# Later rows and weights requested behind an expert's issued scatters, the last multiply in halves, the last tile turned inside the products ahead

## What is computed

```python
x = x + tanh(g_xattn[0]) * xattn(layernorm(x), ctx)     # softmax over 64 masked keys, then @ Wo + bo
xf = layernorm(x)
probs = sigmoid(xf @ gate_w.T)
top_vals, sel = top_k(probs, 2)
weights = top_vals / (top_vals.sum(-1) + 1e-6)
ranks = cumsum(onehot(sel))[sel] - 1                    # place in the expert's list
valid = ranks < 320
padded[expert, rank] = xf                               # rows gathered by expert
h = gelu(padded @ w1[e]); y = h @ w2[e]
x = x + tanh(g_ffn[0]) * sum_k weights_k * y[slot_k]    # 0 where the slot is not valid
```

## Time and profile before

| | |
|---|---|
| median of 3 executions | 338.8 us (338.32 to 339.88) |
| the profiled execution, its own time | 339.9 us |
| its span in the profile | 338.2 us |
| busy share of the span: PE, PEld, DVE, ACT, POOL | 91%, 79%, 74%, 61%, 57% |
| bytes moved by DMA | 45.68 MB, mean 135 GB/s |

### The profile page before, as it was taken

One profiled execution on the slowest core, in us unless ns is written; L12 is line 12 of the kernel. 1 busy time (PEld: TensorE's weight loads), 2 busy tenths in 40 slices (PEclk: granted clock), 3 DMA queues, 4 the chain that ended last, 5 costly groups with the idle time before them and its releaser, 6 DMA issues. The chain is left out here.

```text
span 338.2 us, 6265 instructions
## 1 busy us (share of the span) xinstructions
PE 308.3 (91%) x2077; PEld 267.3 (79%) x2080; DVE 251.2 (74%) x585; ACT 207.9 (61%) x570; POOL 191.4 (57%) x242
## 2 busy tenths in 40 slices
PE   8989999999999999998849999999999999999800
PEld 3646779988888888887724899999999999999700
DVE  2679887698989898989755398888888888887200
ACT  2646877887888888866461376666666666665300
POOL 8034566585777777788771023555555555566650
PEclk9999999999999999999978999999999999999965
DMA  6989999700111111111224737878787878853440
GB/s 159 274 241 292 182 167 152 195 19 16 49 49 55 57 57 64 56 51 62 78 95 149 249 104 201 204 205 208 204 216 211 224 202 220 211 82 43 48 46 8
DMA packets 40906, 45.68 MB, mean 135 GB/s; under 512 B 5461, under 2 KB 34666, under 8 KB 40874
## 3 DMA queue, kind: packets, MB, share of 16 engines
q1 hardware_dynamic: 33410, 35.78, 39.3%
q0 software_dynamic: 7424, 9.48, 15.6%
q10 hardware_dynamic: 40, 0.02, 0.0%
HBM read 28.02 MB, written 17.24 MB: 134 GB/s over the span
## 5 line engine op out<-in xcount | busy, mean ns | idle before, releaser
L554 POOL DMA_INDIRECT out_dram<-wqT,diag x48 | 73.3, 1528 | 77.4 <-DMA out_dram<-wqT,diag 43.4
L1370 PE MATMUL ps_scores<-value_t,score_t 128*128 128x320 f32 x384 | 59.1, 310 | 0.0
L1370 PEld LDWEIGHTS ps_scores<-value_t,score_t 128*128 128x128 f32 x384 | 56.5, 188 | 0.4 <-DVE value_t L1079 0.3
L1269 PE MATMUL ps_out<-value_t,pT 128*128 128x256 f32 x384 | 53.3, 289 | 0.9 <-DVE pT L968 0.9
L1240 PE MATMUL ps_scores<-score_t,xn 128*128 128x512 f32 x192 | 53.9, 426 | 0.0
L1269 PEld LDWEIGHTS ps_out<-value_t,pT 128*128 128x128 f32 x384 | 47.7, 189 | 1.7 <-issue 1.6
L1240 PEld LDWEIGHTS ps_scores<-score_t,xn 128*128 128x128 f32 x192 | 36.4, 190 | 6.8
L713 ACT ACTIVATE ps_scores<-ps_scores 128x640 f32<-128x640 f32 x30 | 20.6, 688 | 34.2 <-PE ps_scores L1370 34.1
L460 POOL DMA_INDIRECT padded<-z,slot_row x32 | 33.4, 1043 | 10.0 <-issue 7.1
L640 ACT ACTIVATE probs<-ps_scores,row_low 128x64 f32<-128x64 f32 x128 | 38.0, 327 | 0.5 <-DVE row_low L941 0.5
L1093 DVE CAST value_t<-ps_scores 128x640 fp32r<-128x640 f32 x30 | 24.7, 824 | 18.0 <-ACT ps_scores L713 17.8
(11 more groups left out here) (210 smaller groups left out, 690.0 us busy)
## 6 DMA issues: line engine op xcount, KB each, us to landing
raw<-in_L_ffn_w_dram SPq DMA_DIRECT2D x16, 512.0 KB, 4.8
wo_sb<-in_L_ffn_w_dram SPq DMA_DIRECT2D x16, 512.0 KB, 3.5
padded<-empty SPq DMA_DIRECT2D x2, 2064.0 KB, 31.0
diag<-padded SPq DMA_DIRECT2D x16, 258.0 KB, 4.9
out_dram<-x SPq DMA_DIRECT2D x16, 128.0 KB, 1.7
padded<-empty SPq DMA_DIRECT2D x1, 1032.0 KB, 34.1
diag<-padded SPq DMA_DIRECT2D x16, 64.5 KB, 4.7
wq_sb<-in_L_xattn_Wq_dram SPq DMA_DIRECT2D x2, 512.0 KB, 8.0
```

Of the source, the lines that this page charges most:

```text
L554: pool.indirect_dma_start(out, bass.IndirectOffsetOnAxis(ap=xg[0:SLOTS[k], r, k, TOKEN:TOKEN + 1].bitcast(U32), axis=0), y[0:SLOTS[k], j, ...
L1269: op = pe.matmul(ps_attn, pT[:, a, c], mv, start=c == 0 and (a, b) == PARTS[0], stop=c == HC - 1 and (a, b) == PARTS[-1])
L1370: op = pe.matmul(ps_scores[:, f, 0:CAPACITY], w1_hl(p, a)[:, c, f * P:(f + 1) * P], x_hl(p, b)[:, c], start=c == 0 and (a, b) == PARTS[0], ...
```

## The change

It has four parts.

1. **Requests of SP.** In a step e >= 1 SP first waits on a new semaphore `issued` until POOL has issued the three scatters of expert e-1 (POOL writes one column of `sent` behind them), then requests the rows of expert e+3, then w1 of expert e+4, then w2 of expert e+3. In the steps before that, w1 goes ahead of w2. The tail part of the rows counts on a semaphore of its own, `tailed`, which PE's turn doesn't wait for. The 64 third rows of expert 0 are requested by ACT.
2. **The last multiply in halves.** The probabilities of tile 15 are multiplied by their norm on POOL in two halves of 8 heads (`last_multiply`) in place of one multiply on DVE, and the norm is made in halves (`last_norm`). PE turns them in two halves.
3. **The last tile turned and counts made inside the products ahead.** `turn_probs(15)` and `counts(6)` stand inside the products of tile 14, `turn_x1(14)` and `router(14)` inside those of tile 15, which write another bank (ps_misc), read copies of their own (`pT_last`) and don't wait for tile 14's residual. Filler multiplies go from 5 and 3 to 2.
4. **The norms from tile 12 on.** DVE makes the negated mean and the variance plus epsilon (two small instructions in `second_stats`), POOL only the reciprocal root, and ACT the shift (`shift`). POOL's `second_norm(14)` and `second_norm(15)` stand between the dispatches of pair 6; one `mark_tokens` stands a step earlier. On DVE the token weights (`weigh`) are computed behind the counts' inputs, and `first_residual(14)` goes behind the placing of pair 6.

```diff
             def expert(e, j, i):
 
+                if e >= 1:
+                    sp.wait_ge(issued, e)
+                    fetch(e + 3)
+                n = e + 4
+                if 2 <= n < EXPERTS:
+                    sp.wait_ge(w1_low, n - 1)
+                    sp.dma_start(raw1[:, n % 2], w1_load[n]).then_inc(w1_loaded[n % 2], 16)
                 n = e + 3
                 if 2 <= n < EXPERTS:
                     sp.wait_ge(w2_low, n - 1)
                     sp.dma_start(raw2[:, n % 2], w2_load[n]).then_inc(w2_loaded[n % 2], 16)
-                n = e + 4
-                if 2 <= n < EXPERTS:
-                    sp.wait_ge(w1_low, n - 1)
-                    sp.dma_start(raw1[:, n % 2], w1_load[n]).then_inc(w1_loaded[n % 2], 16)
-                if e >= -1:
+                if -1 <= e < 1:
                     fetch(e + 3)
...
                     pool.indirect_dma_start(out, ...).then_inc(added[j], 16)
+                if e < EXPERTS - 1:
+                    pool.memset(sent[:, e:e + 1], 0.0).then_inc(issued, 1)
...
+            def last_multiply(h):
+                p, at = LAST % 2, 8 * h
+                pool.wait_ge(norm_ready, TILES + h)
+                pool.tensor_tensor(probs[:, p, at:at + 8], probs[:, p, at:at + 8],
+                                   norm[:, p, at:at + 8, None].to_broadcast([P, 8, KEYS]), ALU.mult).then_inc(normed, 1)
+
             dispatch(PAIRS - 3, 0, (0,))
+            last_multiply(0)
             second_norm(LAST - 2)
+            last_multiply(1)
             dispatch(PAIRS - 3, 0, (1,))
             dispatch(PAIRS - 3, 1)
             mark_tokens(PAIRS - 2)
             mark_tokens(PAIRS - 1)
+            pool.wait_ge(slots_ready, PAIRS - 1)
+            dispatch(PAIRS - 2, 0, (0,))
             second_norm(LAST - 1)
-            pool.wait_ge(slots_ready, PAIRS - 1)
-            dispatch(PAIRS - 2, 0)
-            dispatch(PAIRS - 2, 1)
+            dispatch(PAIRS - 2, 0, (1,))
+            dispatch(PAIRS - 2, 1, (0,))
             second_norm(LAST)
+            dispatch(PAIRS - 2, 1, (1,))
...
-            keep_busy(5)
-            attend(LAST - 1, {HC // 2: lambda: router(LAST - 2)})
-            turn_probs(LAST)
-            counts(PAIRS - 2)
-            turn_x1(LAST - 1)
-            keep_busy(3)
-            attend(LAST, {HC // 2: lambda: router(LAST - 1)})
+            keep_busy(2)
+            router(LAST - 2)
+            attend(LAST - 1, {HC // 2: lambda: turn_probs(LAST), HC - 1: lambda: counts(PAIRS - 2)})
+            attend(LAST, {3: lambda: turn_x1(LAST - 1), HC - 2: lambda: router(LAST - 1)})
```

More of the change, by code:

```diff
@@ L273, in build @@
         fetched = [sem(f"fetched{k}") for k in range(GATHERS)]
+        tailed = [sem(f"tailed{k}") for k in range(GATHERS)]
         added = [sem(f"added{k}") for k in range(2)]
@@ L539, in _ @@
                 dispatch(PAIRS - 1, k)
-            pool.memset(sent[:, :], 0.0).then_inc(rows_sent, 1)
+            pool.memset(sent[:, EXPERTS - 1:], 0.0).then_inc(rows_sent, 1)
             for k in range(2):
@@ L598, in _, with copy_probs @@
                 job(n, *JOBS[n])
-            def copy_probs(t):
-                for h in range(2):
+            def copy_probs(t, halves=(0, 1)):
+                for h in halves:
                     act.wait_ge(turned, 2 * t + h + 1)
-                    if h == 0:
+                    if t == LAST:
+                        act.wait_ge(scored, 2 * TILES)
+                    elif h == 0:
                         wait(act, attended, t)
-                    act.activation(pT[:, 0, 4 * h:4 * h + 4].rearrange("p c n -> p (c n)"), ps_pT[:, h],
+                    act.activation(pT_of(t, 0)[:, 4 * h:4 * h + 4].rearrange("p c n -> p (c n)"), ps_pT[:, h],
                                    ACT.Copy).then_inc(p_high, 1)
@@ L612, in second_rows @@
                 act.wait_ge(ln2_ready, t + 1)
+                bias = l2[:, p, 2:3]
+                if t >= LATE_TILE:
+                    bias = shift[:, p]
+                    act.activation(bias, l2[:, p, 2:3], ACT.Copy, scale=l2[:, p, 1:2]).then_inc(shifted, 1)
+                    act.wait_ge(shifted, t - LATE_TILE + 1)
                 if t >= RING:
@@ L705, in expert @@
                 if e == -1:
+                    for k in range(2):
+                        act.wait_ge(dispatched[k], 64 * PAIRS // 2)
+                    act.dma_start(xg[0:SLOTS[2], 0, 2], padded[2 * P:CAPACITY, :]).then_inc(fetched[0], 16)
                     for t in range(2):
@@ L891, in step @@
                 if exists(t3):
[L892 to L893 removed]
+                    if t3 < LATE_TILE:
+                        wait(dve, ln2_ready, t3 - 1)
+                        dve.bn_aggr(mv2[:, p3], stats2[:, :]).then_inc(stats2_ready, 1)
+                    else:
+                        second_stats(t3)
                 if route:
@@ L1213, in turn_probs @@
                 for h in range(2):
+                    if t == LAST and h == 1:
+                        pe.wait_ge(normed, TILES + 1)
                     wait(pe, p_low, 2 * (t - 1) + h + 1)
@@ L1259, in attend @@
             def attend(t, between):
-                wait(pe, x1_ready, t)
+                if t < LAST:
+                    wait(pe, x1_ready, t)
                 for c in range(HC):
@@ L1268, in attend @@
                         mv = value_w[b][:, batch_of(t), c]
-                        op = pe.matmul(ps_attn, pT[:, a, c], mv, start=c == 0 and (a, b) == PARTS[0],
+                        op = pe.matmul(attn_of(t), pT_of(t, a)[:, c], mv, start=c == 0 and (a, b) == PARTS[0],
                                        stop=c == HC - 1 and (a, b) == PARTS[-1])
@@ L1314, in step @@
                 if counted_here and r >= LATE_PAIR:
-                    between[HC - 2] = lambda: counts(r)
+                    between[HC // 2 + 1] = lambda: counts(r)
                 if exists(s - 2):
```

101 lines of the change are left out of this document (62 added, 39 removed).

## The result

The changed kernel took **341.4 us** (median of 17 executions, 339.52 to 343.27), the kernel before beside it 339.4 (17 executions, 338.29 to 341.62): ratio 1.0055, 95% interval 1.0039 to 1.0071. It is slower by about half a per cent; the forecast was 336.0 and a range of 334.8 to 338.4. The profiled execution is one of the best: 339.91 us, span 338.1, mean granted clock 0.967. So two things are to be explained: why even this execution is no faster than that of before (339.9, span 338.2, clock 0.968), and why the median lies 1.5 above it.

The account below looks back on a forecast made before the run. POOL's scatter queue, running behind a full PE, was taken to end last, with filler setting the experts' start. Profiled 339.9 - 2.3 - 0.5 = 337.1, or 336.0 us against the median of 338.8; range 334.8 to 338.4.

Parts of the forecast that it names:

- I take the quiet period of 7.56 to 7.72 for all experts: POOL's scatters: with loads requested behind them, every expert's scatters would repeat as fast as at the quiet end.
- it is below 8.22, so the lag goes in a few experts: POOL's scatters: a period shorter than PE's 8.22 us would let them catch up with the results.
- the first term: SP's requests behind issued scatters: expert 15 scatters at 321.8 against 324.07, so -2.3 us; bounds 0 and -2.7.
- expert 13 scatter at the end of ACT's result (306.6): Late experts: expert 13 scatters when its result is there, expert 14 at 314.2, expert 15 at 321.8.
- the loads meet the scatters: Rival: gaps ahead of scatters are 3.3 instead of 2.4, period 8.5, first term 0; 338.3 us, chance 0.17.
- The second term, -0.5,: Norms at the routing's end: last count 0.6 us earlier, so filler and first rows' turn come earlier; bounds 0 and -2.7.
- an early rise of the clock: Filler ahead of the first rows' turn: if the clock rises early, only the rows' landing holds; bound -2.7 us.
- They end 1.5 to 1.9 later ... 0: Products of tiles 14 and 15: tile 14's end later, tile 15's follow at once and end near 168.7; effect 0.
- a clock that stays up: Rival: PE's clock stays up or rises early, so the landing at 183.5 decides the turn; 334.9 us, chance 0.10.
- Late loads, PE waiting for weights (+5.5): Rival: PE waits for rows or weights, 0.5 us in each of 12 experts, less 0.5; about 344 us, chance 0.06.

Follow-up runs that it names:

- The two runs with the longer program: Kernel before with only the new requests, SP's wait and memsets, plus 96 already met waits in PE's program: 339.60 us (1.0013), then 339.81 us (1.0016).
- the fillers: Changed kernel plus filler multiplies around the turns of the last three tiles and ahead of the counts' halves: 337.27 us (0.9956), then 336.70 us (0.9932).

## Why the prediction was wrong

**"I take the quiet period of 7.56 to 7.72 for all experts"** is the step that failed. I took it from the end of the loop, where no DVE operation with two SBUF inputs is running as a scatter starts. The wait did get short (2.4 to 2.5), so that loads requested behind an issued scatter do let it land, as argued. But a scatter on time issues in 2.10 and not in 1.57, so the period is 8.2, and "it is below 8.22, so the lag goes in a few experts" turned into no margin at all. There was no lag to work off at first, since the first wait of 5.50 was no longer there; but once late landings had added to it, it stayed at 1.9 us or more. By the time from expert 0's first scatter to expert 15's (124.3 against 123.4) the first term came out as +0.9 in the trace of the changed kernel, instead of -2.3.

**The size was too large even without late landings.** The two runs with the longer program show the full effect, 122.1 and 122.2 against 123.4: -1.3 us. I let expert 13 scatter at the end of ACT's result (306.6); the least lag is 0.79, which alone is 0.8 of the difference.

**The rival "the loads meet the scatters"** had the size of the gaps right (3.3 forecast, 3.5 to 4.0 behind four odd experts) and the cause wrong: only every second expert has them, and the same loads go without them in the run with the longer program. What delays these landings stays open. Its mechanism is real, though: without SP's wait the loads do meet the scatters, for +10 us.

**The second term, -0.5,** was about right in the profiled execution: the last count at 174.59 (forecast 174.4), the rows turned 0.80 earlier, the routing's last dispatch ending at 178.59 (177.63 + 0.96; forecast 178.5), later than before as said. I had written that 3 us of filler stand behind landed rows, and priced an early rise of the clock from that at -2.7; the fillers bear it out (the rows turned 2.4 us earlier than in the changed kernel).

**"They end 1.5 to 1.9 later ... 0"** is the second step that failed. The turn of x1 of tile 14 came 2.4 us later than before (166.73 against 164.33), and not 1.5. And I looked at when the products end, and not at what PE does meanwhile: it idles in 155 to 160 and 165 to 170, the fillers there were cut, and behind that idle time the clock falls early in many executions, for +1.6 us; with fillers in these places it held in both traces. I had a rival for a clock that stays up and none for one that falls earlier. I did cite the Trainium skill (TensorE: Matmul & The Clock Gate, "What's actually happening") for a turn of the clock that varies between executions; the runs agree, with medians 1.5 us apart for the same kernel in two comparisons, and I should have let it widen the range upward.

**Late loads, PE waiting for weights (+5.5):** did not come. PE is busy for 118.95 us of 200 to 340, before 119.64.

**What I missed altogether** is the requests' real worth: they take away a feedback of which the median of before shows nothing. With the fillers it shows, and then it is 10 us.

## What to carry to other kernels

A queue that runs behind the bottleneck engine keeps a delay unless its period, *measured on time and with its neighbours running*, is clearly below the bottleneck's; read that period where the neighbours run, not in the quiet tail. When work is moved so that PE idles elsewhere, count its idle time stretch by stretch before and after and put fillers in the new holes, and size a filler that stands ahead of a landing for the clock it will really have. Look at all executions and not at the median alone: a kernel with rare executions 2 to 5% longer may be next to a feedback, and a change that removes it can show no gain until something else is changed.

## What was not expected of the hardware

The issue of an indirect DMA waits for the end of a DVE operation with two SBUF inputs that it finds running, and for none that starts later: up to 1.05 us more of issue, read in 160 of 960 issues.

PE's instruction loads are DMA packets of 16 KB among the data (17 in the span, queue 8, 0.9 to 1.8 us each on one engine), and with nothing but PE's program made longer by 96 met waits the scatters' waits behind odd experts fell from 2.8 to 3.6 down to 2.4 to 2.5 us. In the changed kernel's trace the load at 214 us lies over a request of SP that took 2.1 us to issue instead of 0.5 and over the wait of 4.02:

```profile
q8 instruction: 1, 0.02, 10.1%
```

```profile
214.30 2.09 SPq L393 DMA_DIRECT2D diag<-padded  x1
```

(first the DMA view of 214 to 215 us, packets, MB and share of 16 engines: one packet of 1.6 us; then SP's timeline.) Whether a met wait costs time stays open. Only 24 of the 96 stand ahead of tile 13's turn, which came at 158.22 and 158.27 with them and at 157.76 and 156.92 without: 0.5 and 1.3 us, where two executions of one kernel are 0.8 apart.
